# Weight columns turned to rows by VectorE's 32x32 blocks instead of TensorE, with VectorE's slot reordered

## The reference

```python
qk = X @ Wqk; q, k = jnp.split(qk, 2, axis=-1); v = X @ Wv
agg = jnp.einsum('bij,bjd->bid', adj, k * mask[:, :, None])
w = inv_scale * mask * jnp.einsum('bid,bid->bi', q, agg)       # one weight per node
x = layernorm(X + softmax(w, axis=1)[:, :, None] * v)          # layer 0

query, keyt, value = x @ Wq.T + bq, x @ Wk.T + bk, x @ Wv.T + bv
weight = adj * jnp.exp(jnp.einsum('bqd,bkd->bqk', query, keyt))
weight = weight / jnp.sum(weight, axis=2, keepdims=True)
out = layernorm(x + jnp.einsum('bqk,bkd->bqd', weight, value)) # layer 1
```

## Time and profile before

| | |
|---|---|
| median of three runs | 293.14 us |
| the profiled execution | 292.77 us |
| its span in the profile | 291.0 us |
| mean granted clock of TensorE | 0.997 |
| busy share TensorE, VectorE, ScalarE, GpSimd | 97%, 87%, 82%, 75% |
| HBM traffic | 107 GB/s over the span |

### The profile page before, as it was taken

One profiled execution on the slowest core, in us unless ns is written; L12 is line 12 of the kernel. 1 busy time (PEld: TensorE's weight loads), 2 busy tenths in 40 slices (PEclk: granted clock), 3 DMA queues, 4 the chain that ended last, 5 costly groups with the idle time before them and its releaser, 6 DMA issues.

```text
span 291.0 us, 7075 instructions
## 1 busy us (share of the span) xinstructions
PE 283.4 (97%) x1984; PEld 263.7 (91%) x1984; DVE 253.9 (87%) x783; ACT 238.2 (82%) x568; POOL 217.4 (75%) x269
## 2 busy tenths in 40 slices
PE   8999999999999999999999999999999999999991
PEld 7789999999999999999999999999999999999980
DVE  1478999999989999999998999899999999999784
ACT  3455779899888989988898998889899888987862
POOL 1556987778898778789887788987787898877331
PEclk9999999999999999999999999999999999999998
DMA  7931323333334423334433333444233344210112
GB/s 241 332 97 37 91 93 127 93 91 98 106 125 126 126 93 88 99 100 126 126 124 95 88 99 100 126 126 126 94 87 96 103 126 126 90 57 26 46 38 108
DMA packets 19165, 31.26 MB, mean 107 GB/s; under 512 B 2128, under 2 KB 6608, under 8 KB 19152
## 3 DMA queue, kind: packets, MB, share of 16 engines
q1 hardware_dynamic: 19152, 31.11, 34.7%
HBM read 22.71 MB, written 8.39 MB: 107 GB/s over the span
## 4 chain that ended last, share of the span: by engine, by line
PE 96%; issue 1%; DVE 1%; POOL 0%; POOLq 0%; ACT 0%; DVEq 0%
PE ps L890 25%; PE ps L891 25%; PE ps L892 25%; PE ps L993 9%; PE ps L973 5%; PE ps L941 1%; PE ps L1112 1%; PE ps L913 1%; PE ps L1117 1%; PE ps L998 1%; PE ps L1126 1%; DVE x L661 0%; PE ps L952 0%; PE ps L960 0%; POOLq L42 0%
## 5 line engine op out<-in xcount | busy, mean ns | idle before, releaser
L890 PE MATMUL ps<-w_hi,xt_hi 128*128 128x512 f32 x124 | 49.3, 398 | 0.0
L891 PE MATMUL ps<-w_lo,xt_hi 128*128 128x512 f32 x124 | 48.6, 392 | 0.0
L892 PE MATMUL ps<-w_hi,xt_lo 128*128 128x512 f32 x124 | 48.3, 390 | 0.0
L372 POOL TENSOR_TENSOR edge_lo<-edge,edge_hi 128x256 fp32r<-128x256 f32 x29 | 21.6, 743 | 34.5 <-ACT edge_hi L544 34.5
L461 ACT ACTIVATE x<-x_sum,shift,rstd 128x256 f32<-128x256 f32 x60 | 32.8, 595 | 15.3 <-POOL shift L386 15.3
L305 POOL TENSOR_TENSOR x1b<-x,bv_all 128x512 f32<-128x512 f32 x31 | 39.7, 1282 | 2.9 <-DVE x L823 2.0
L359 POOL TENSOR_TENSOR xt_lo<-xt_raw,xt_hi 128x512 fp32r<-128x512 f32 x31 | 40.1, 1294 | 1.8 <-ACT xt_hi L443 1.8
L383 POOL TENSOR_TENSOR rstd<-var_eps,minus_half 128x4 f32<-128x4 f32 x31 | 31.6, 1018 | 9.0 <-DVE var_eps L799 9.0
L890 PE MATMUL ps<-x1t_hi,at_hi 128*128 128x256 f32 x124 | 37.4, 302 | 0.0
L366 POOL TENSOR_TENSOR x_lo<-x_raw,x_hi 128x512 fp32r<-128x512 f32 x28 | 36.2, 1294 | 0.0
L890 PE MATMUL ps<-wv_hi,x1t_hi 128*128 128x258 f32 x124 | 35.5, 286 | 0.0
(11 more groups left out here) (166 smaller groups left out, 909.5 us busy)
## 6 DMA issues: line engine op xcount, KB each, us to landing
xt_raw<-xt_pairs SPq DMA_DIRECT2D x32, 256.0 KB, 2.7
x_raw<-x_pairs SPq DMA_DIRECT2D x32, 256.0 KB, 2.7
out_pairs<-x SPq DMA_DIRECT2D x31, 256.0 KB, 2.0
adjt<-adjt_pairs SPq DMA_DIRECT2D x32, 129.0 KB, 2.1
p<-params SPq DMA_DIRECT2D x1, 770.0 KB, 6.7
p<-params SPq DMA_DIRECT2D x1, 512.0 KB, 3.8
p<-params SPq DMA_DIRECT2D x1, 256.0 KB, 4.6
out_pairs<-x SPq DMA_DIRECT2D x2, 128.0 KB, 1.8
```

What stands on the lines that cost most here:

```text
L890: nc.tensor.matmul(out, s_hi, m_hi, start=first, stop=False)
L891: nc.tensor.matmul(out, s_hi, m_lo, start=False, stop=False)
L892: return nc.tensor.matmul(out, s_lo, m_hi, start=False, stop=last)
```

## The change

For pairs 3 to 30 the columns of w are turned to rows by VectorE instead of TensorE. `w_col` becomes 32 columns wide (30 of them zeroed once by GpSimd), and `transpose_w` on VectorE writes four 32x32 blocks into a new SBUF tile `w_row`, of which rows 0 and 1 are used. `row_max` follows directly, ahead of `den_inv`, and it and ScalarE's exp read SBUF instead of PSUM for these pairs. TensorE no longer transposes w for them. In VectorE's slot the statistics of `x1_sum` go ahead of `edge`, and the statistics of `x2` go from behind the x2 updates of slot t to behind `edge` of slot t+1. `bias_scores` goes to ScalarE, behind val_hi. ScalarE's x_hi goes from the end of slot t-1 to behind xt_hi in slot t.

```diff
-        w_col = sb("w_col", [128, 2])
+        w_col = sb("w_col", [128, BLOCK])
+        w_row = sb("w_row", [BLOCK, NODES])
+        def w_rows(r):
+            return w_row_ps(r) if by_tensor(r) else w_row[0:2, :]
...
+            nc.gpsimd.memset(w_col[:, :], 0.0)
...
+            def bias_scores(u):
+                act.wait_ge(score_exp_done, u)
+                nc.scalar.activation(score_bias[:, :], val_ps[:, :, DIM], ACT.Identity, bias=s_bias[:, 0:1])\
+                    .then_inc(score_bias_done, 1)
...
-                if r == 0:
-                    split_x(4, 4)
+                if exists(t + 3) and r + 3 >= SPLIT:
+                    split_x(t + 3, r + 3)
...
-                    nc.scalar.activation(exp_row_ps(r + 2), w_row_ps(r + 2), ACT.Exp, bias=neg_max[:, 0:1],
+                    nc.scalar.activation(exp_row_ps(r + 2), w_rows(r + 2), ACT.Exp, bias=neg_max[:, 0:1],
...
-                if exists(t + 4) and r + 4 > SPLIT:
-                    split_x(t + 4, r + 4)
+                    if r != DRAIN:
+                        bias_scores(t)
...
+            def transpose_w(u, r):
+                for g in range(2):
+                    dve.wait_ge(w_done[g], u + 1)
+                dve.wait_ge(row_exp_done, u)
+                for b in range(0, NODES, BLOCK):
+                    block = nc.vector.transpose(w_row[:, b:b + BLOCK], w_col[b:b + BLOCK, :])
+                block.then_inc(w_row_done, 1)
...
             def slot(t, r):
...
                     sum_x1(t + 1, r + 1)
+                if exists(t + 1):
+                    for g in range(2):
+                        dve.wait_ge(x1_sum_done[g], t + 2)
+                    both_stats(0, x1_sum[(r + 1) % 2]).then_inc(stats1_done, 1)
                 if exists(t - 1):
...
                     nc.vector.tensor_tensor(edge[:, :], exp_s[:, :], adjt[(r - 1) % 4][:, 0:PAIR_N], ALU.mult)\
                         .then_inc(edge_done, 1)
-                if exists(t + 1):
-                    for g in range(2):
-                        dve.wait_ge(x1_sum_done[g], t + 2)
-                    both_stats(0, x1_sum[(r + 1) % 2]).then_inc(stats1_done, 1)
+                if exists(t - 2):
+                    dve.wait_ge(x2_done, t - 1)
+                    both_stats(1, x2[(r - 2) % 4]).then_inc(stats2_done, 1)
...
                         weight(t + 2, r + 2, g)
+                    if not by_tensor(r + 2):
+                        transpose_w(t + 2, r + 2)
+                        row_max(t + 2, r + 2)
...
-                        if g == 1 and exists(t + 2):
+                        if g == 1 and exists(t + 2) and by_tensor(r + 2):
                             row_max(t + 2, r + 2)
...
-                if exists(t - 1):
+                if r == DRAIN:
                     dve.wait_ge(x2_done, t)
                     both_stats(1, x2[(r - 1) % 4]).then_inc(stats2_done, 1)
...
-                if exists(t) and r != DRAIN:
-                    if r == 0:
-                        dve.wait_ge(biases_ready, 1)
-                    bias_scores(t)
...
-                    queries(x1t_hi, x1t_lo, (t + 2, r + 2) if exists(t + 2) and r > 0 else None)
+                    queries(x1t_hi, x1t_lo, (t + 2, r + 2) if r > 0 and by_tensor(r + 2) else None)
```

More of the change, by code:

```diff
@@ L611, in weight @@
             def weight(u, r, g):
+                if r == 0:
+                    dve.wait_ge(consts_ready, 1)
                 dve.wait_ge(agg_copied, u + 1)
@@ L761, in drain @@
                                             ALU.add, ALU.mult).then_inc(last_out_done, 1)
+            def transpose_w(u, r):
[5 more added lines that the diff above has]
+                block.then_inc(w_row_done, 1)
             def row_max(u, r):
                 dve.wait_ge(w_row_done, u + 1)
-                nc.vector.tensor_reduce(neg_max[:, :], w_row_ps(r), AX.X, ALU.max, negate=True).then_inc(row_max_done, 1)
+                nc.vector.tensor_reduce(neg_max[:, :], w_rows(r), AX.X, ALU.max, negate=True).then_inc(row_max_done, 1)
             def slot(t, r):
@@ L940, in transpose_w @@
                     pe.wait_ge(w_done[g], u + 1)
-                nc.tensor.transpose(w_row_ps(r), w_col[:, :], ident[:, :]).then_inc(w_row_done, 1)
+                nc.tensor.transpose(w_row_ps(r), w_col[:, 0:2], ident[:, :]).then_inc(w_row_done, 1)
             def transpose_p(u, r):
```

## The result

The changed kernel takes 294.64 us (median of 5 runs, 294.23 to 294.91) against 293.14 us for the kernel before beside it (292.75 to 293.27): a ratio of 1.0058, 95% interval [1.0047, 1.0069]. It is slower by 0.6%, 1.5 us. The forecast was 297.8, slower by 1.6%: the direction holds, the size is about three times too large. The profiled execution took 294.91 us, with a span of 292.8 us.

A forecast was written before the change was run, and what follows sets the result against it. TensorE bounds the kernel before; the change makes VectorE the bound, 8.68 us per slot against TensorE's 8.37. 292.77 plus 5.3 (28 slots times 0.19) is 298.1, less about 0.3 of slack: 297.8 us, range 289.3 to 301.2.

The forecast's parts named there:

- Rival 1: The four w_col blocks on VectorE overlap, about 0.41 us; TensorE stays the bound, 289.5 us; chance 0.23.
- neg_mean's stall: VectorE's neg_mean, held up by GpSimd's edge_lo: 0.11 us in place of 0.44, giving back 0.33 per slot.
- rival 4: neg_mean's stall on VectorE stays because edge_lo comes later too: 0.2 us more per slot, 303 us; chance 0.06.
- Rival 3: GpSimd stalls the new VectorE blocks as it does neg_mean: 0.36 us more per slot, 308 us; chance 0.05.
- the sum of VectorE's slot, 8.68: VectorE's new slot from start-to-start distances: 8.60 us plus 0.08 for the loop turn, 0.19 over the old slot.
- both weight reductions to the second accumulator read 0.96: VectorE's stretch behind x1t_lo, carried over from the old slot at 0.96 us, bringing the running sum to 4.83.
- the blocks' 0.82: Four w_col transpositions on VectorE: 0.82 us, between bounds 0.68 and 0.90; named the most fragile term.
- At each turn of the loop ... In a slot without slack it counts, 0.08 per slot: VectorE idles 0.32 us for issue once in four slots; hidden before, now 0.08 us per slot.
- den_inv to x: VectorE's distance from the reciprocal den_inv to the x update, late in the slot: 0.31 us.
- x_sum to its statistics: Start of VectorE's slot: second x_sum update 0.39 us after the first, then 0.52 until the x1_sum statistics.
- rival 2: Even: VectorE's slot is 8.49 us, blocks at low bound 0.68, loop turn hidden; 292.6 to 293.7; chance 0.08.
- TensorE's own stream: Removing one w_col transposition per slot from the query product saves TensorE 0.12 us: slot 8.37, 3.3 us over 28.

The follow-up runs named there:

- two_blocks: Changed kernel with two of the four w_col blocks left out, half of each row of weights staying zero: 290.71 us, ratio 0.9939 to the kernel before.
- after_extra_dense: Changed kernel with an additional VectorE maximum over 128 columns between val_lo and neg_mean in slots 1 to 28: 299.80 us, ratio 1.0233 to the kernel before.
- edge_first: Changed kernel with edge ahead of the statistics of x1_sum again, those of x2 staying behind both: 298.40 us, ratio 1.0190 to the kernel before.
- bias_on_vector: Changed kernel with bias_scores back on VectorE at the end of its slot: 296.85 us, ratio 1.0129 to the kernel before.
- blocks_only: Kernel before with only the four blocks on VectorE and the row maximum right behind them: 306.19 us, ratio 1.0459 to the kernel before.
- rows_by_tensor: Changed kernel with TensorE turning w for all pairs and the maximum between the x2 updates as before: 293.45 us, ratio 1.0022 to the kernel before.
- fewer_waits: Changed kernel less three VectorE waits (first x1_sum, first w_done, row_exp_done): 290.87 us, ratio 0.9935 to the kernel before.
- den_first: Changed kernel with the reciprocal den_inv between the second weight reduction and the four blocks: 291.08 us, ratio 0.9938 to the kernel before.
- fewer_and_den: Changed kernel with both den_inv moved ahead of the blocks and the three waits left out: 290.40 us, ratio 0.9914 to the kernel before.

## Why the prediction was wrong in size

**Right.** VectorE became the bound, and with that the kernel slower; two_blocks and after_extra_dense show it from both sides. The blocks stand in single file at 0.20 each: four and the step to the maximum take 0.87, forecast 0.85. Rival 1 (they overlap) is out. The Trainium skill, "VectorE: DVE Perf Modes", section "Two Vector instructions with no wait between them", had them held by their inputs' changing quadrants; the trace agrees, 0.21 from start to start for a duration of 0.20. neg_mean's stall gave back what I said and a little more, so rival 4 is out; it was close, since edge_lo (132.19 to 132.93) ends only 0.13 behind neg_mean's start. Rival 3 is out too: GpSimd's x_lo is at work beside the blocks from 134.43 to 135.72 and they show no 0.36; the Trainium skill, "GPSIMD Engine Reference", section "Specifications", limits the contention to two-port modes and two SBUF inputs, and edge (two SBUF inputs) in edge_first, with 0.80 for 0.41, agrees. neg_mean has one input; whether its mode is a two-port one, no row here tells.

**Wrong: the sum of VectorE's slot, 8.68 for a measured 8.525.** Against TensorE-bound 8.49 that made 0.19 per slot where 0.04 was right. The terms:
- *"both weight reductions to the second accumulator read 0.96"*: they take 0.81. In the old slot the second reduction started 0.55 behind the first; after the change 0.40 (133.54 to 133.94). The missing 0.15 had been a wait for TensorE's `project`. Its last matmul in the kernel before and in two_blocks, each a timeline of TensorE:

```profile
106.65 0.39 PE L892 MATMUL ps<-w_hi,xt_lo 128*128 128x512 f32 x1
```

```profile
131.02 0.40 PE L914 MATMUL ps<-w_hi,xt_lo 128*128 128x512 f32 x1
```

It ends at 107.04 and 131.42, and the second reduction starts at 107.17 and, in the timeline of VectorE below, at 131.55: 0.13 behind in both. Where VectorE is the bound, the product has long ended and the wait is nil, under the same three wait instructions (in the changed kernel it ends at 133.56, 0.38 ahead of the second reduction). I had noted among the fragile points, behind the blocks' 0.82, that a start-to-start distance could hold a wait that goes away; this was one, and I had looked for it at edge, den_inv and the maximum, but not here.

```profile
131.55 0.48 DVE L630 CUSTOM_DVE_ANT_0 agg<-ps,agg,adjt 128x256 f32<-128x256 f32 x1 [0.20 <-issue]
```

- *"At each turn of the loop ... In a slot without slack it counts, 0.08 per slot"*: no slot of the changed kernel has that gap. Its x_sum starts 0.97 behind the first p_col block in three slots of four and 0.90 in the fourth. The moved bias_scores alone does not explain it: bias_on_vector and blocks_only have that instruction back behind the blocks and no such gap either, and rows_by_tensor, where TensorE is the bound, has none without it. What the gap needs stays open.
- neg_mean 0.07 for 0.11 and den_inv to x 0.26 to 0.28 for 0.31, another 0.08 too much.
- In the other direction, x_sum to its statistics 0.98 for 0.91, the 0.07 at x_sum in three slots of four, and 0.04 at the blocks. That is 0.16 in all. fewer_waits took 0.12 out again at two of these places, the statistics and the blocks; x_sum stayed at 0.97 there.

Together: 0.16 less 0.15, 0.08 and 0.08 is -0.15, and 8.68 becomes 8.53. The two terms that failed, the weight reductions and the turn of the loop, are 0.23 of what was too much, 0.31 in all; it is chance that the terms that were too small, 0.16, took back half of it.

**Signs that misled.** I had said that the chain would go over to VectorE, that VectorE would be busy above 95% in the loop, that TensorE would be idle before its scores or its attention products, and that slots would take 8.6 to 8.75. None of this came: the chain is TensorE for 95%, VectorE is busy in 31.61 of 33.96 us (93%), TensorE's records show no idle there, and the slot is 8.525. That VectorE is the bound rests on the experiments. Of the rivals, rival 2 (even, 292.6 to 293.7) ended nearer to the measured time than my forecast; the turn of the loop is hidden as it supposed, but the blocks are not at its low 0.68.

**Off, with less weight.** TensorE's own stream came down by 0.08, not 0.12, to 8.407 (two_blocks, den_first, fewer_and_den); 0.04 of what one transposition took is not given back. Matmuls of the query product lie 0.120 apart in the changed kernel and about 0.118 before; the cause stays open. And 0.3 us in slot 0 was no part of the sum. Against 8.49 only VectorE's 8.525 mattered, so the first of these moved the forecast little.

## What to carry to other kernels

Where two engines need nearly the same time per round, the second one's round can't be read off the first one's trace: for each distance that is to be carried over, ask whether it ends with a wait on the engine that is about to lose its lead, and take that wait out. A page that says TensorE 97% busy and a chain that is all TensorE are no proof that it is the bound: TensorE's busy time here covered its waits. What told was two blocks less and one instruction more, the latter put where the engine has no gap. And before a step is moved between engines for good, close the gaps on the engine that gets it: with den_inv moved and three waits less, the same change is not 0.6% slower but 0.9% faster (290.40, [0.9901, 0.9927]) than the kernel before.

## What the runs showed of the hardware

- Two of VectorE's instructions, edge with its two SBUF inputs (0.80 for 0.41) and the small neg_mean from SBUF to SBUF (0.52 for 0.16), stand still until the GpSimd instruction in work ends. The blocks from SBUF (0.84 for four beside x_lo) do not. The order on VectorE decides which of GpSimd's instructions the two meet; one step in the order was worth 4 us.
- A further wait of VectorE costs even where it changes nothing in the order of work: 0.07 us at the statistics (one wait left out, ahead of the one that comes last) and 0.05 at the blocks (two left out, one on either side of it), 3.6 us for both places in 28 slots. Which of the three costs how much was not told apart.
- A 32x32 block takes 200 ns from SBUF and 207 from PSUM, and successive ones do not overlap (0.84 and 0.87 us for four).
